# Attention with row maxima found ahead: another order of pieces, scores and sums in the unit loop, and one wait for each ACT and DVE instruction

## The chip, the cores and the metric

The kernel runs on one core of a Trainium2 chip. The metric is the time of one execution in device microseconds (us). The engines are named as in the profile: PE is TensorE's matmuls, PEld its weight loads, DVE is VectorE, ACT is ScalarE, POOL is GpSimd, SP is the engine that issues most DMAs. Each engine runs its own instructions in order, and they wait for each other by semaphores.

## What is computed

One block of a transformer with a layer norm in front of two branches: attention with 16 heads of 16 dimensions over 4096 positions in 2 batch rows, and a feed-forward branch with butterfly transforms. Cut to what matters:

```python
# x: (2, 4096, 256), W_qkv: (256, 768)
xn = layernorm(x)
qkv = (xn @ W_qkv + b_qkv).reshape(B, D, 3, 16, 16).transpose(2, 0, 3, 1, 4)
q, k, v = qkv
scores = softmax(einsum("bhip,bhjp->bhij", q, k), axis=-1)     # 32 x 4096 x 4096
attn = einsum("bhij,bhjp->bhip", scores, v).reshape(B, D, 256)
h = butterfly(xn @ W_exp + b_exp, up_weights)                  # 1024 wide, 10 stages
h = gelu(h + up_bias)
y = butterfly(h, down_weights) @ W_con + b_con + down_bias
return x + attn + y
```

The softmax subtracts the true maximum of each row, so the kernel needs each row's maximum before it can take the exponentials.

## The kernel before

**Stages.** First come the layer norm, q, k and v (to about 270 us), then the attention, which holds over 85% of the time, then the feed-forward branch from about 5294 us. The change touches the attention alone.

**Tiles and units.** The queries of a head are taken 2048 at a time (`QB`); there are 64 such rounds (`SUPER`). A round is worked on twice. As 16 *tiles* of 128 queries it goes through the search for maxima: q times all 4096 keys in 8 *pieces* of 512 keys (`PIECES`), each a matmul into one bank of PSUM. As 16 *units* it goes through the softmax proper: each unit multiplies two blocks of 128 keys (half 0 and half 1) with the 2048 queries in 8 *scores* of 512 columns (`score`, L843), ACT takes their exponentials (`exp`, L646), and PE multiplies these with v (`sums`, L857, four matmuls for each half, each run as two instructions). The maxima are ahead of the units by 21 tiles (`AHEAD`), so the loop over 1024 units does in step u the pieces of tile n = u + 21, the scores of unit u + 1 and the sums of unit u. The first 18 tiles (`PAIRED`) are done in another way ahead of the loop; the last 21 units have no pieces.

**Pieces.** DVE reduces a piece to its maximum over 512 keys (`reduce_piece`, L708). To save DVE one piece in eight, one bank holds a *difference*: q times (last keys of one half less those of another), matmul with `k_diff`. ACT takes its relu into `spill` (`rectify`, L670), and DVE adds that to the *merged* piece while it reduces it (L704): a + relu(b - a) is the larger of both. `DIFFERENCE` and `MERGED` say at which places of `PIECE` these stand (3 and 6 before; the difference at place 3 is that of the next tile, n + 1). A piece has 48 rows and a score 50, so each lies in the upper or the lower half of the PE array (`lower`), and two matmuls of different halves run side by side. The sums use all 128 rows.

**Banks.** Four banks hold scores in turn (a score waits for the exponential four before it), three banks hold pieces in turn (`use`, `bank_of`, `free_region`): each piece waits until the use three before it has been read. One bank holds the sums.

**Order in a step of PE before** (lines 885 to 905): piece 0, score 0, piece 1, scores 1 and 2, piece 2, score 3, sums of half 0; then the difference of the next tile, piece 4, scores 4 and 5, piece 5, scores 6 and 7, the merged piece 6, piece 7, sums of half 1. ACT's order is four exponentials, a relu, four exponentials. `SCORE` gives each score its half and its 512 queries. The engines' orders are written out by hand; no planner is at work.

**Once in 16 steps.** When a round's maxima are complete, DVE negates them and splits them into two bf16 parts (`negate`, `high_part`, `low_part`, L723, L728, L732) in the tile with n % 16 = 1, PE transposes them at n % 16 = 2 (`neg_to_rows`, L830; it takes a turn of the three banks), DVE copies them (`copy_rows`, L741) and SP places them under q. When a round's sums are complete, DVE transposes them behind the tile with n % 16 = 4 (`turn`, L747), and takes a reciprocal in the next (`invert`, L751); POOL scales and adds.

**Waits.** An instruction of ACT or DVE that waits for two semaphores is preceded by an instruction that waits for the first alone. Before, that is so for the exponentials of the first 512 queries of each half (sums of two units ago, then the score), for the relu (the merged piece of two tiles ago, then the difference) and for the merged reduction (the relu, then the piece).

Of the kernel before, what the change touches and what calls it, by code (L numbers as in the profile page):

```python
# [44 lines left out]
def attention_and_butterfly_ffn(nc, x, w_qkv, b_qk_columns, b_v, w_exp, b_exp, up_planes, up_bias_columns, down_planes,  # L45
# [13 lines left out]
    QG = QB // BANK  # L59
# [8 lines left out]
    UNITS = KT // 2  # L68
# [21 lines left out]
    with ExitStack() as ctx:  # L90
# [350 lines left out]

        PIECE = [(1, 0), (1, 1), (0, 0), (1, 2), (0, 1), (0, 2), (1, 3), (0, 3)]
        DIFFERENCE, MERGED = 3, 6


        SCORE = [(r // 2 % 2, 2 * (r // 4) + r % 2) for r in range(2 * QG)]
        LAST_OF_HALF = [max(r for r in range(2 * QG) if SCORE[r][0] == h) for h in range(2)]

# [13 lines left out]
        for n in range(PAIRED):  # L462
            for i in range(0, PAIRS_OF_TILE, 2):
                for what in ("apart", "second"):
                    for pair in (i, i + 1):
                        use((n, what, pair), what == "second")
        use((PAIRED, DIFFERENCE), False)
        for n in range(PAIRED, TILES_ALL + TURN_TILE + 1):
            if n % QT == TURN_TILE:
                use(("neg", n // QT - 1), True)  # L470
            for j in range(PIECES if n < TILES_ALL else 0):
                if j != DIFFERENCE:
                    use((n, j), True)
                elif n + 1 < TILES_ALL:
                    use((n + 1, j), False)
        vector_uses, scalar_uses = list(accumulate(by_vector)), list(accumulate(by_scalar))
# [40 lines left out]
        with nc.Block() as block:  # L517
# [122 lines left out]
            def _(act):  # L640
                def exp(u, r):
                    half, g = SCORE[r]
                    if g == 0 and u >= 2:
                        act.wait_ge(s_pv, 2 * (u - 2) + half + 1)
                    act.wait_ge(s_score, 2 * QG * u + r + 1)
                    nc.scalar.activation(probs[:, 2 * (u % 2) + half, BANK * g:BANK * g + BANK],  # L646
                                         ps_s[:, r % 4, :], ACT.Exp).then_inc(s_exp, 1)
# [18 lines left out]
                def rectify(n):  # L666
                    act.wait_ge(s_diff_ps, spilled(n))
                    if n >= PAIRED + 2:
                        act.wait_ge(s_region_free, vector_uses[use_of[n - 2, MERGED]])
                    nc.scalar.activation(spill[:, n % 2, :], region(use_of[n, DIFFERENCE]), ACT.Relu).then_inc(s_spilled, 1)  # L670
# [7 lines left out]
                act.wait_ge(s_ones_in, 16 * 4)  # L678
                for r in range(QG):
                    exp(0, r)  # L680
                rectify(AHEAD)
                for r in range(QG, 2 * QG):
                    exp(0, r)
                for u in range(UNITS_ALL):
                    if u + 1 < UNITS_ALL:
                        for r in range(QG):
                            exp(u + 1, r)
                    if u + AHEAD + 1 < TILES_ALL:
                        rectify(u + AHEAD + 1)
                    if u + 1 < UNITS_ALL:  # L690
                        for r in range(QG, 2 * QG):
                            exp(u + 1, r)

            @block.vector
            def _(dve):
                def reduce_piece(n, j):
# [4 lines left out]
                    if j == MERGED:  # L701
                        dve.wait_ge(s_spilled, spilled(n))
                        dve.wait_ge(s_region, vector_uses[use])
# [75 lines left out]
            def _(pe):  # L779
# [27 lines left out]
                def piece(n, j):  # L807

                    if j == DIFFERENCE:
                        n += 1  # L810
                    if n >= TILES_ALL:
# [35 lines left out]
                def sums(u, half):  # L847

                    s, at = divmod(u, UNITS)
                    head = s // 2  # L850
                    if at == 0 and half == 0:
                        if s > 0:
                            pe.wait_ge(s_o_free, s)
                        pe.wait_ge(s_vc[head % 2], 16 * (head // 2 + 1))
                    pe.wait_ge(s_exp, 2 * QG * u + LAST_OF_HALF[half] + 1)
                    for g in range(QG):
                        last = nc.tensor.matmul(ps_o[VW * g:VW * g + VW, :], v_cols[:, KT * (head % 2) + UNITS * half + at, :],  # L857
                                                probs[:, 2 * (u % 2) + half, BANK * g:BANK * g + BANK],
                                                start=(at == 0 and half == 0), stop=(at == UNITS - 1 and half == 1))
                    last.then_inc(s_pv, 1)  # L860
# [3 lines left out]
                for n in range(PAIRED):  # L864
                    for i in range(0, PAIRS_OF_TILE, 2):
                        pairs(n, i)
                piece(PAIRED - 1, DIFFERENCE)
                for n in range(PAIRED, AHEAD):
# [15 lines left out]
                for u in range(UNITS_ALL):  # L884
                    n = u + AHEAD
                    if n % QT == TURN_TILE and n // QT <= SUPER:
                        neg_to_rows(n // QT - 1)
                    piece(n, 0)
                    score(u + 1, 0)
                    piece(n, 1)  # L890
                    score(u + 1, 1)
                    score(u + 1, 2)
                    piece(n, 2)
                    score(u + 1, 3)
                    sums(u, 0)
                    piece(n, 3)
                    piece(n, 4)
                    score(u + 1, 4)
                    score(u + 1, 5)
                    piece(n, 5)  # L900
                    score(u + 1, 6)
                    score(u + 1, 7)
                    piece(n, 6)
                    piece(n, 7)
                    sums(u, 1)

# [235 lines left out]
```

## Time and profile before

| | |
|---|---|
| runs | 5672.61 us median of 3 (5670.88 to 5674.43) |
| profiled execution | 5674.86 us, of which the span of instructions is 5673.1 us |
| PE, DVE, ACT busy | 5605.1 (99%), 4884.6 (86%), 4977.2 (88%) us |
| POOL busy | 524.8 us (9%) |
| exponentials (L646) | 8192 x 608 ns, 4222.6 us busy |
| reductions (L708) | 6036 x 686 ns, 3966.7 us busy |
| merged reductions (L704) | 1006, 684.8 us busy |
| relus (L670) | 1006 x 597 ns, 601.0 us busy |
| granted TensorE clock | mean 0.992 of full |

A group's busy time is less than its count times its mean, since an engine begins an instruction before the last has quite ended: exponentials in a row start some 0.48 us apart though each takes 0.61. A busy PE is a PE that has some matmul under way, which says little of how full it is. By slices of the span, all three engines are at 90% or more from the third or fourth fortieth to the thirty-seventh: the attention looks the same from end to end.

### The profile page before, as it was taken

What the parts mean: (1) busy time and instruction counts of PE and PEld (TensorE: products, weight loads), DVE (VectorE), ACT (ScalarE), POOL (GpSimd) and SP (SyncE); (2) the same over time, 40 slices, a digit from 0 to 9 for tenths busy, and PEclk for the clock granted to TensorE, in tenths of its full rate; (3) what the DMA queues carried; (4) which work ended last, traced back from release to release, by engine and by line L of the source; (5) the groups of instructions that cost most, each with busy time, mean ns of one, the idle gap of its engine ahead of it and who ended that gap; (6) DMA issues with size and microseconds to landing.
All of it is one profiled execution on the core that took longest, in us unless ns stands there. A gap on an engine that the chain in (4) does not pass through costs nothing. (4 is left out here: it accounts for less than half of the span.)

```text
span 5673.1 us, 97332 instructions
## 1 busy us (share of the span) xinstructions
PE 5605.1 (99%) x35880; PEld 2613.5 (46%) x35880; DVE 4884.6 (86%) x9104; ACT 4977.2 (88%) x9651; POOL 524.8 (9%) x482
## 2 busy tenths in 40 slices
PE   8799999999999999999999999999999999999999
PEld 5444444444444444444444444444444444444698
DVE  6689999999999999999999999999999999996233
ACT  3489999999999999999999999999999999999544
POOL 2245564000000000000000000000000000000000
PEclk9889999999999999999999999999999999999999
DMA  8611111000000000000000000000000000000111
GB/s 288 200 43 43 50 54 42 21 21 19 14 16 21 21 21 21 15 21 21 21 18 14 16 21 21 21 20 16 21 21 21 17 12 20 21 21 2 34 44 41
DMA packets 232761, 197.02 MB, mean 35 GB/s; under 512 B 171752, under 2 KB 192616, under 8 KB 220520
## 3 DMA queue, kind: packets, MB, share of 16 engines
q1 hardware_dynamic: 228848, 168.00, 10.4%
q0 software_dynamic: 3456, 23.07, 1.4%
q8 instruction: 268, 4.39, 0.3%
q14 instruction: 189, 1.55, 0.1%
HBM read 128.07 MB, written 60.82 MB: 33 GB/s over the span
## 5 line engine op out<-in xcount | busy, mean ns | idle before, releaser
L646 ACT ACTIVATE probs<-psum 128x512 f32<-128x512 f32 x8192 | 4222.6, 608 | 294.8 <-PE psum L843 292.8
L708 DVE TENSOR_REDUCE maxima<-psum 128x1 f32<-128x512 f32 x6036 | 3966.7, 686 | 364.7 <-PE psum L821 255.6
L821 PE MATMUL psum<-k_rows,q_rows 48*128 48x512 f32 x7042 | 2494.3, 455 | 0.6 <-ACT spill L670 0.6
L857 PE MATMUL psum<-probs,v_cols 128*32 128x512 f32 x16384 | 2184.7, 605 | 0.5
L843 PE MATMUL psum<-q_rows,k_rows 50*128 50x512 f32 x8192 | 2061.2, 424 | 0.0
L821 PEld LDWEIGHTS psum<-k_rows,q_rows 48*128 48x128 f32 x7042 | 1176.6, 184 | 1248.8 <-DVE maxima L704 809.6
L843 PEld LDWEIGHTS psum<-q_rows,k_rows 50*128 50x128 f32 x8192 | 1266.5, 186 | 135.0 <-ACT probs L646 44.5
L704 DVE CUSTOM_DVE_ANT_0 merged<-psum,spill 128x512 bf16<-128x512 f32 x1006 | 684.8, 681 | 2.7 <-issue 1.9
L670 ACT ACTIVATE spill<-psum 128x512 f32<-128x512 f32 x1006 | 601.0, 597 | 23.9 <-PE psum L821 23.6
L857 PEld LDWEIGHTS psum<-probs,v_cols 128*32 128x32 f32 x16384 | 323.3, 108 | 622.0 <-issue 325.8
L821 PEld LDWEIGHTS psum<-k_diff,q_rows 48*128 48x128 f32 x1006 | 184.6, 183 | 843.0 <-DVE maxima L708 787.7
L821 PE MATMUL psum<-k_diff,q_rows 48*128 48x512 f32 x1006 | 498.5, 496 | 0.2 <-DVE maxima L708 0.2
L583 POOL TENSOR_TENSOR o_t<-o_t,recip 128x256 f32<-128x256 f32 x64 | 39.6, 618 | 4527.8 <-DVE recip L751 4527.8
L1049 ACT ACTIVATE gelus<-psum,bias_up 128x512 f32<-128x512 f32 x128 | 88.3, 690 | 189.4 <-PE psum L1013 187.6
L296 ACT ACTIVATE parts<-psum,bqk 128x512 fp32r<-128x512 f32 x64 | 59.0, 922 | 133.8 <-PE psum L406 102.6
L1091 DVE TENSOR_TENSOR hidden_low<-gelus,hidden_high 128x512 fp32r<-128x512 f32 x128 | 88.6, 692 | 100.9 <-ACT hidden_high L1052 100.9
L406 PE MATMUL psum<-xnt,wqkv 128*128 128x512 f32 x256 | 121.3, 619 | 29.7 <-DVE parts L345 28.5
L1025 PE MATMUL psum<-w_down_high,hidden_low 128*128 128x256 f32 x512 | 145.0, 283 | 0.0
L1025 PE MATMUL psum<-w_down_low,hidden_high 128*128 128x256 f32 x512 | 145.0, 283 | 0.0
L1025 PE MATMUL psum<-w_down_high,hidden_high 128*128 128x256 f32 x512 | 144.9, 283 | 0.0
L1097 DVE TENSOR_TENSOR y<-psum,y 128x1024 f32 (+1 forms) x16 | 19.6, 1225 | 125.0 <-PE psum L1025 125.0
L747 DVE STREAM_TRANSPOSE o_t<-psum 128x512 f32<-128x512 f32 x64 | 45.2, 706 | 74.8 <-PE psum L857 74.8
(94 smaller groups left out, 2067.0 us busy)
## 6 DMA issues: line engine op xcount, KB each, us to landing
q_rows<-q_parts SPq DMA_DIRECT2D x128, 256.0 KB
q_parts<-parts SPq DMA_DIRECT2D x32, 512.0 KB, 6.0
k_parts<-parts SPq DMA_DIRECT2D x32, 512.0 KB, 3.7
k_rows<-k_parts SPq DMA_DIRECT2D x64, 256.0 KB
q_rows<-q_parts SPq DMA_DIRECT2D x128, 128.0 KB
planes<-in_up_planes POOLq DMA_DIRECT2D x10, 1024.0 KB, 11.3
planes<-in_down_planes POOLq DMA_DIRECT2D x10, 1024.0 KB, 5.4
y<-in_x SPq DMA_DIRECT2D x16, 512.0 KB, 6.0
```

The source lines that it names most:

```text
L296: nc.scalar.activation(in_chunk_order(m, parts[:, PARTS * m, :]), from_chunk(m), ACT.Identity, bias=bqk[:, m:m + 1]).then_inc(s_high, 1)
L406: last = nc.tensor.matmul(ps_qk[:, m, :], wqkv[:, k, P * m:P * m + P], xnt[:, KD * p + k, :], start=(k == 0), stop=(k == KD - 1))
L646: nc.scalar.activation(probs[:, 2 * (u % 2) + half, BANK * g:BANK * g + BANK], ps_s[:, r % 4, :], ACT.Exp).then_inc(s_exp, 1)
L670: nc.scalar.activation(spill[:, n % 2, :], region(use_of[n, DIFFERENCE]), ACT.Relu).then_inc(s_spilled, 1)
L704: nc.vector.tensor_tensor_reduce(merged[:, :], region(use), spill[:, n % 2, :], 1.0, LOWEST, ALU.add, ALU.max, accum_out=largest).then_inc ...
L708: nc.vector.tensor_reduce(largest, region(use), axis=AX_X, op=ALU.max).then_inc(s_region_free, 1)
L821: nc.tensor.matmul(region(use_of[n, j]), q_rows[m % 4][lower:lower + ROWS, P * t:P * t + P], keys[lower:lower + ROWS, :], start=True, stop ...
L843: nc.tensor.matmul(ps_s[:, r % 4, :], k_rows[s // 2 % 2][lower:lower + ROWS + MAX_PARTS, key:key + P], q_rows[s % 4][lower:lower + ROWS + ...
L857: last = nc.tensor.matmul(ps_o[VW * g:VW * g + VW, :], v_cols[:, KT * (head % 2) + UNITS * half + at, :], probs[:, 2 * (u % 2) + half, BAN ...
L1025: last = nc.tensor.matmul(ps_d[:, t, 0:D], h[:, m, P * t:P * t + P], w[:, m, :], start=(m == 0 and n == 0), stop=(m == HT - 1 and n == 2))
L1049: nc.scalar.activation(gelus[:, m % 2, :], ps_h[:, m % 4, :], ACT.Gelu, bias=bias_up[:, 1, m:m + 1]).then_inc(s_h, 1)
L1091: nc.vector.tensor_tensor(hidden_low[:, m, :], gelus[:, m % 2, :], hidden_high[:, m, :].bitcast(F32), ALU.subtract).then_inc(s_h_low, 1)
```

## The change

Three things are altered, all in the attention.

The order within a step of the unit loop: the difference stands first and belongs to the same tile (`DIFFERENCE` is 0), so a step is difference, pieces 1 and 2, scores 0 to 3, pieces 3 and 4, sums of half 1; then piece 5, scores 4 and 5, the merged piece 6, piece 7, scores 6 and 7, sums of half 0. `SCORE` now takes the halves in turn, half 1 first, and `PIECE` is permuted to match. ACT's order is the relu and then eight exponentials.

The waits: the exponential no longer waits for the sums of two units ago, the relu no longer for the merged reduction of two tiles ago, the merged reduction no longer for the relu. In the new order PE issues the score behind those sums, the difference behind a piece that waited for that merged reduction, and the merged piece behind a piece that waited for the relu.

The sums of unit u start their accumulation with half 1 and end it with half 0.

```diff
--- before.py
+++ after.py
@@ -439,11 +439,11 @@
         ps_o = psum[:, 7, :]
 
 
-        PIECE = [(1, 0), (1, 1), (0, 0), (1, 2), (0, 1), (0, 2), (1, 3), (0, 3)]
-        DIFFERENCE, MERGED = 3, 6
-
-
-        SCORE = [(r // 2 % 2, 2 * (r // 4) + r % 2) for r in range(2 * QG)]
+        PIECE = [(1, 2), (0, 0), (1, 0), (1, 1), (0, 1), (0, 2), (1, 3), (0, 3)]
+        DIFFERENCE, MERGED = 0, 6
+
+
+        SCORE = [(1 - r % 2, r // 2) for r in range(2 * QG)]
         LAST_OF_HALF = [max(r for r in range(2 * QG) if SCORE[r][0] == h) for h in range(2)]
 
 
@@ -464,15 +464,11 @@
                 for what in ("apart", "second"):
                     for pair in (i, i + 1):
                         use((n, what, pair), what == "second")
-        use((PAIRED, DIFFERENCE), False)
         for n in range(PAIRED, TILES_ALL + TURN_TILE + 1):
             if n % QT == TURN_TILE:
                 use(("neg", n // QT - 1), True)
             for j in range(PIECES if n < TILES_ALL else 0):
-                if j != DIFFERENCE:
-                    use((n, j), True)
-                elif n + 1 < TILES_ALL:
-                    use((n + 1, j), False)
+                use((n, j), j != DIFFERENCE)
         vector_uses, scalar_uses = list(accumulate(by_vector)), list(accumulate(by_scalar))
 
         def region(n):
@@ -640,8 +636,6 @@
             def _(act):
                 def exp(u, r):
                     half, g = SCORE[r]
-                    if g == 0 and u >= 2:
-                        act.wait_ge(s_pv, 2 * (u - 2) + half + 1)
                     act.wait_ge(s_score, 2 * QG * u + r + 1)
                     nc.scalar.activation(probs[:, 2 * (u % 2) + half, BANK * g:BANK * g + BANK],
                                          ps_s[:, r % 4, :], ACT.Exp).then_inc(s_exp, 1)
@@ -665,8 +659,6 @@
 
                 def rectify(n):
                     act.wait_ge(s_diff_ps, spilled(n))
-                    if n >= PAIRED + 2:
-                        act.wait_ge(s_region_free, vector_uses[use_of[n - 2, MERGED]])
                     nc.scalar.activation(spill[:, n % 2, :], region(use_of[n, DIFFERENCE]), ACT.Relu).then_inc(s_spilled, 1)
 
                 minus_k()
@@ -676,19 +668,13 @@
                 for n in range(PAIRED, AHEAD):
                     rectify(n)
                 act.wait_ge(s_ones_in, 16 * 4)
-                for r in range(QG):
-                    exp(0, r)
-                rectify(AHEAD)
-                for r in range(QG, 2 * QG):
+                for r in range(2 * QG):
                     exp(0, r)
                 for u in range(UNITS_ALL):
+                    if u + AHEAD < TILES_ALL:
+                        rectify(u + AHEAD)
                     if u + 1 < UNITS_ALL:
-                        for r in range(QG):
-                            exp(u + 1, r)
-                    if u + AHEAD + 1 < TILES_ALL:
-                        rectify(u + AHEAD + 1)
-                    if u + 1 < UNITS_ALL:
-                        for r in range(QG, 2 * QG):
+                        for r in range(2 * QG):
                             exp(u + 1, r)
 
             @block.vector
@@ -699,7 +685,6 @@
                     column = COLUMNS * (n % QT) + j - (j > DIFFERENCE)
                     largest = maxima[:, n // QT % 2, column:column + 1]
                     if j == MERGED:
-                        dve.wait_ge(s_spilled, spilled(n))
                         dve.wait_ge(s_region, vector_uses[use])
                         nc.vector.tensor_tensor_reduce(merged[:, :], region(use), spill[:, n % 2, :], 1.0, LOWEST,
                                                        ALU.add, ALU.max, accum_out=largest).then_inc(s_region_free, 1)
@@ -806,8 +791,6 @@
 
                 def piece(n, j):
 
-                    if j == DIFFERENCE:
-                        n += 1
                     if n >= TILES_ALL:
                         return
                     m, t = divmod(n, QT)
@@ -848,7 +831,7 @@
 
                     s, at = divmod(u, UNITS)
                     head = s // 2
-                    if at == 0 and half == 0:
+                    if at == 0 and half == 1:
                         if s > 0:
                             pe.wait_ge(s_o_free, s)
                         pe.wait_ge(s_vc[head % 2], 16 * (head // 2 + 1))
@@ -856,7 +839,7 @@
                     for g in range(QG):
                         last = nc.tensor.matmul(ps_o[VW * g:VW * g + VW, :], v_cols[:, KT * (head % 2) + UNITS * half + at, :],
                                                 probs[:, 2 * (u % 2) + half, BANK * g:BANK * g + BANK],
-                                                start=(at == 0 and half == 0), stop=(at == UNITS - 1 and half == 1))
+                                                start=(at == 0 and half == 1), stop=(at == UNITS - 1 and half == 0))
                     last.then_inc(s_pv, 1)
 
                 pe.wait_ge(s_k[0], 16 * K_LOADS)
@@ -864,7 +847,6 @@
                 for n in range(PAIRED):
                     for i in range(0, PAIRS_OF_TILE, 2):
                         pairs(n, i)
-                piece(PAIRED - 1, DIFFERENCE)
                 for n in range(PAIRED, AHEAD):
                     if n == QT + TURN_TILE:
                         neg_to_rows(0)
@@ -885,24 +867,21 @@
                     n = u + AHEAD
                     if n % QT == TURN_TILE and n // QT <= SUPER:
                         neg_to_rows(n // QT - 1)
-                    piece(n, 0)
-                    score(u + 1, 0)
-                    piece(n, 1)
-                    score(u + 1, 1)
-                    score(u + 1, 2)
-                    piece(n, 2)
-                    score(u + 1, 3)
-                    sums(u, 0)
+                    for j in range(3):
+                        piece(n, j)
+                    for r in range(QG):
+                        score(u + 1, r)
                     piece(n, 3)
                     piece(n, 4)
+                    sums(u, 1)
+                    piece(n, 5)
                     score(u + 1, 4)
                     score(u + 1, 5)
-                    piece(n, 5)
+                    piece(n, 6)
+                    piece(n, 7)
                     score(u + 1, 6)
                     score(u + 1, 7)
-                    piece(n, 6)
-                    piece(n, 7)
-                    sums(u, 1)
+                    sums(u, 0)
```

## Rows read from the trace of the kernel before

**Rows 1.** Waits of the whole span: engine, line, releaser: us in total, times, longest.
```profile
PEld psum L821 <- DVE maxima L708: 830.2, 1097, 1.7
...
PEld psum L821 <- ACT spill L670: 354.7, 939, 1.1
...
ACT probs L646 <- PE psum L843: 292.8, 1005, 1.8
```

**Rows 2.** Busy time in four stretches of a unit (length, then each engine).
```profile
3004.15:3005.90 1.75, 1.75 (x14) 1.02 (x10) 1.47 (x3) 1.75 (x5) 0.00 (x0) 1.00 0.00 0
3005.90:3006.90 1.00, 1.00 (x11) 0.16 (x10) 1.00 (x4) 1.00 (x3) 0.00 (x0) 1.00 0.00 0
3006.90:3008.03 1.13, 1.13 (x12) 0.72 (x8) 1.01 (x2) 0.85 (x3) 0.00 (x0) 1.00 0.00 0
3008.03:3009.02 0.99, 0.99 (x9) 0.15 (x8) 0.99 (x3) 0.99 (x4) 0.00 (x0) 1.00 0.00 0
```

**Rows 3.** Timeline, first stretch: start, us, engine, line, operation [idle before].
```profile
3004.16 0.50 PE L821 MATMUL psum<-k_diff,q_rows 48*128 48x512 f32 x1
...
3004.69 0.60 ACT L670 ACTIVATE spill<-psum 128x512 f32<-128x512 f32 x1
3004.73 0.69 DVE L708 TENSOR_REDUCE maxima<-psum 128x1 f32<-128x512 f32 x1 [0.28 <-PE psum L821]
...
3005.34 0.31 PEld L821 LDWEIGHTS psum<-k_rows,q_rows 48*128 48x128 f32 x2 [0.39 <-ACT spill L670]
...
3005.47 0.50 PE L821 MATMUL psum<-k_rows,q_rows 48*128 48x512 f32 x1
```

**Rows 4.** Timeline of the rest of that unit.
```profile
3006.01 0.68 DVE L704 CUSTOM_DVE_ANT_0 merged<-psum,spill 128x512 bf16<-128x512 f32 x1
...
3006.62 2.69 DVE L708 TENSOR_REDUCE maxima<-psum 128x1 f32<-128x512 f32 x4
...
3006.90 0.50 PE L843 MATMUL psum<-q_rows,k_rows 50*128 50x512 f32 x1
...
3007.52 0.60 ACT L646 ACTIVATE probs<-psum 128x512 f32<-128x512 f32 x1 [0.28 <-PE psum L843]
3007.70 0.39 PE L843 MATMUL psum<-q_rows,k_rows 50*128 50x512 f32 x1
```

**Rows 5.** Timeline where maxima are negated and turned, DVE and PE.
```profile
1929.00 0.26 DVE L723 TENSOR_REDUCE neg_max<-maxima 128x16 f32<-128x112 f32 x1
...
1929.77 0.16 DVE L728 CAST neg_parts<-neg_max 128x16 bf16<-128x16 f32 x1
1929.94 0.69 DVE L708 TENSOR_REDUCE maxima<-psum 128x1 f32<-128x512 f32 x1
...
1932.00 0.22 PE L830 MATMUL psum<-ident_bf,neg_parts 128*32 128x128 bf16 x1
1932.15 0.49 PE L821 MATMUL psum<-k_rows,q_rows 48*128 48x512 f32 x1
...
1932.58 0.50 PE L821 MATMUL psum<-k_rows,q_rows 48*128 48x512 f32 x1
```

**Rows 6.** Timeline where a round's sums are transposed, DVE and PE.
```profile
2025.36 0.71 DVE L747 STREAM_TRANSPOSE o_t<-psum 128x512 f32<-128x512 f32 x1
2025.99 1.25 DVE L708 TENSOR_REDUCE maxima<-psum 128x1 f32<-128x512 f32 x2
2027.16 0.23 DVE L751 RECIPROCAL recip<-o_t 128x16 f32<-128x16 f32 x1
...
2027.15 0.49 PE L821 MATMUL psum<-k_diff,q_rows 48*128 48x512 f32 x1
2027.29 0.49 PE L821 MATMUL psum<-k_rows,q_rows 48*128 48x512 f32 x1
```

**Rows 7.** Line 830: count, duration ns min/median/max, first and last start.
```profile
L830 PE MATMUL psum<-ident_bf,neg_parts x64: 218/219/286, 284.7 to 5213.2; 128*32 128x128 bf16 x64
```

**Rows 8.** Timeline at the start of the loop, PE.
```profile
298.46 0.80 PE L821 MATMUL psum<-k_rows,q_rows 48*128 48x512 f32 x2 [0.56 <-ACT spill L670]
```

## The prediction

> **What bounds the kernel now.** I began with the page. PE shows 99%, but its matmuls overlap, so that share says little. ACT (88%) and DVE (86%) come near their limit without reaching it: neither is full. So I went to the table of waits [rows 1]. PE's weight loads wait for DVE's reductions and for ACT's relu; ACT and DVE in turn wait for PE. That is a ring, not one full engine, and one must see which link closes it. Most of the span is 1024 units of 4.87 us, nearly all alike, and a table of busy time over one of them, cut where PE changes its work, shows the ring [rows 2]: 1.75 us for the stretch that begins with the difference piece, 1.00 for a block of sums, 1.13 for the other stretch of pieces and scores, 0.99 for the other sums. Reader: the two sums blocks and the 1.13 us stretch are PE's own time; only the 1.75 us stretch holds a wait.
>
> Inside that stretch [rows 3]: the difference and piece 4 start at 3004.16, DVE starts on piece 4 at 3004.73 (0.57 later), takes 0.69, and 0.05 after its end, at 3005.47, PE starts the last piece, which needed that bank. The sums follow 0.43 later. 0.57 + 0.69 + 0.05 + 0.43 = 1.74. The relu makes a shorter ring beside it: start 3004.69, end 3005.29, piece 6 at 3005.34. The other stretch has four matmuls deep in each half of the array and no live wait; its last matmul, at 3007.70, is followed by the sums 0.32 later [rows 2, 4]. PE's cycle thus has one round trip to DVE in it, and DVE and ACT have two idle spells each.
>
> **The change, part by part. The order in a steady unit.** Call the start of the difference 0. The new stretch A is difference, piece 1, piece 2, four scores, pieces 3 and 4, sums(u, 1); stretch B is piece 5, four scores, pieces 6 and 7 among them, sums(u, 0). There are three banks for eight pieces, so each piece still waits for the one three before it: piece 3 for the relu, piece 4 for the reduction of piece 1. With the durations of rows 3: relu from 0.53 to 1.13, piece 3 at 1.19; reduction of piece 1 from 0.57 to 1.26, piece 4 at 1.31, sums at 1.74. These are the same numbers as now, since the same pair starts the stretch and the same round trip closes it. The sums take 1.00: B starts at 2.74. In B the longer half of the array holds pieces 5 and 7 and two scores, four deep as now: 1.13, sums at 3.87, next unit at 4.86. **Steady gain: nothing**, as long as the waits in B stay covered. DVE's starts are 0.60 to 0.61 apart when it doesn't wait [rows 4] (2.69 less 0.69, less a wait of some 0.2, over three; and 3006.01 to 3006.62), so it takes pieces 1 to 4 at 0.57, 1.17, 1.78 and 2.38, and the last is free at 3.12. Piece 7 wants its bank at about 3.21 if it isn't to come late (its turn in B gives an end at 3.71, and a matmul that waited needs 0.50 [rows 3]). The cover is 0.09 to 0.10 us. Now the same bank has far more: that is the new weak point. The other waits: DVE reaches piece 7 at 4.48 and frees its bank at 5.17, which is 0.31 into the next unit, so piece 2 and the scores behind it start some 0.1 late; the first exponential then starts at 1.10 and the fourth ends near 3.16, 0.2 ahead of the last score of B, which needs it. Nothing of that reaches the sums. A wait missed by d here costs 1003 times d.
>
> **The waits left out.** ACT loses the wait on the sums ahead of the first column block of each half and the wait on a merged piece ahead of the relu, DVE loses the wait on the relu ahead of the merged reduction. Where the instruction isn't starved, the trace gives them no time: DVE's merged reduction follows 0.60 after the reduction ahead of it [rows 3, 4]. Where ACT is starved they show: the first exponential starts 0.12 after its score ends (3006.90 + 0.50 against 3007.52), the relu, whose extra wait was over long before, 0.03 to 0.04 after its matmul [rows 3, 4]. The difference, some 0.06 to 0.09, lies in ACT's idle time (0.28 there [rows 4]), which PE doesn't wait for. So I put it at 0 in the 1003 units with pieces. In the last 21 units, which have no pieces, ACT and PE wait for each other in one ring and it counts once each: 21 x 0.06 = 1.2 us gained; between 0 and 1.9. The Trainium skill, "VectorE: DVE Perf Modes", in "The DRAIN you can't avoid", says that a semaphore with each operation costs nothing extra. By it the last units gain 0, not 1.2 us; for back-to-back work the trace agrees (0.60 with and without the extra wait), for an instruction that is starved it doesn't.
>
> **The stops, once in 16 units.** Here the order matters. (a) Negation of the maxima. Two of DVE's three small operations, the negation and the first split, fall between piece 0 and piece 4; the split's slot is 0.17 (1929.77 to 1929.94), and I take as much for the negation [rows 5]. DVE would idle 0.28 ahead of piece 4 anyway [rows 3], so they are nearly hidden. In the new order they fall between the reductions of pieces 1 and 4, with no idle spell between. Piece 4's bank comes free at 3.12 + 0.34 = 3.46, 0.25 past what piece 7 can bear: that unit is 0.25 longer. (b) The next unit. The transposes take PE 0.15 [rows 5] in either order. Now they cost 0.24 in all: the second piece is at 0.43 after the first (1932.15 to 1932.58) and not 0.34, as it waits for the reduction of the tile before. In the new order that reduction runs late after (a), to 0.18 into this unit, so piece 1 can be loaded at 0.24 and everything that hangs on its round trip is 0.23 late. DVE's copy of the turned rows fits ahead of piece 1. Together 0.48 against 0.24: **0.24 lost**. (c) The transposition of the sums takes a DVE slot of 0.63 [rows 6] (2025.36 to 2025.99). It now falls in DVE's two idle spells: what is left is the 0.14 by which the piece beside the difference is late (2027.15, 2027.29 [rows 6]), some 0.12 in the unit. In the new order it comes between piece 7 and piece 1 of the next tile: slot from 5.09 (0.23 of the next unit) to 0.86, where piece 1 would have been taken at 0.57. A piece that has waited reads a little faster there (two reductions in 1.25 [rows 6]), so piece 4 is 0.24 to 0.29 late; the reciprocal's 0.16 behind piece 1 takes the rest of the cover, 0 to 0.1 more. Taken 0.25, against 0.12: **0.13 lost**. The unit that holds each of these has pieces in 62 of the 64 rounds [rows 7]. 62 x (0.24 + 0.13) = 23 us. Bounds: 62 x 0.1 = 6 us if most is caught up by DVE's idle spells, 62 x 0.55 = 34 us if the backlog costs two units each time.
>
> **The start.** Now one relu of a coming tile is queued behind four exponentials, and PE idles 0.56 us for it [rows 8]. With the difference at the head of its own tile that stall goes, and the relu then queues behind eight exponentials at the first unit, where PE is late at a low clock anyway. Between 3 gained and 1 lost; I take 1 gained. SP's queue isn't moved: its loads wait on counts of exponentials and sums that come in the same units as now.
>
> **The sum**, against the profiled execution: span 5673.1 + 23 - 1.2 - 1 = 5693.9; around the span lie 1.8 us (5674.86), so 5695.7. This execution is 2.3 us over the median of the runs shown (5672.61), which gives a median of **5694 us**, +0.4%.
>
> **The rivals.** (1) No change to measure: the stops are mostly absorbed, since DVE idles 0.6 us in a steady unit in either order, and the start and the tail give 2 back. 5673 + 6 - 2 = 5677. For it: DVE catches up within one unit. Against: the wait for piece 7 comes before DVE's second idle spell. (2) Faster: the extra waits matter in every unit. Mechanism: the last score of stretch A now starts 0.1 late because it waits for the fourth exponential, and the exponentials start late by the extra wait. If it is this link, and not DVE's, that sets the last piece, 0.06 comes back in each of 1003 units: 5673 - 60 + 23 = 5636; with half of it, 5666. It decides if piece 7 now starts by that score and not 0.05 after DVE's reduction; rows 3 speak against it, as the 0.05 is exact. (3) Much slower: the cover of 0.1 for piece 7 isn't there in the steady unit. The price is 1003 us for each us missed: 0.05 gives 5694 + 50 = 5744. It decides if the first four reductions of a unit are ever more than 0.64 apart or the first starts later than 0.67. For it: the cover is small and my starts are good to 0.02 or 0.03 each. (4) The change doesn't take the order it says: excluded, the diff writes each engine's order out.
>
> **How the numbers follow.** Chances: forecast 0.56 (own range 5685 to 5707), rival 1 0.19, rival 2 0.15, rival 3 0.10. 0.2% of 5673 is 11 us, about what a measurement of this kernel can tell from no change: the line is at 5661 and 5684. Rival 1 is within, a third of rival 2 too, with a few hundredths of the forecast's low end: same 0.25. Slower 0.63, faster 0.12. The range: 5660 takes in rival 1 and the weak end of rival 2, 5728 the upper bound of the stops and the weak end of rival 3; about 0.19 is left out, most of it below.
>
> **What would show it.** In the changed trace a steady unit should last 4.86 us, with sums 1.74 and 3.87 after the difference. DVE should idle about 0.3 ahead of piece 1 and 0.3 ahead of piece 5. PE's idle time for the reductions should gather at the last piece of A. The relu should no longer have scores or exponentials between its matmul and it. ACT should start 0.04 after a score that it waited for, not 0.12. The rounds of 16 units should be 78.5 us apart instead of 78.1. If a steady unit differs from 4.86 by more than 0.02, the main step is wrong: longer by a wait of piece 7 means rival 3, shorter means that PE's ring isn't what I took it for. If the unit holds and the rounds stay at 78.1, rival 1 is right.

## The result, and the profile after

The changed kernel takes 5689.64 us (median of 9 runs, 5686.55 to 5691.74) against 5672.61 (median of 9, 5668.83 to 5674.91): 17 us more, ratio 1.0030, 95% interval 1.0021 to 1.0039. The prediction was 5694.

| us | before | after |
|---|---|---|
| span of the profiled execution | 5673.1 | 5687.8 |
| start of the last matmuls of the sums | 5288.9 | 5303.1 |
| mean unit, 1500 to 4500 us | 4.884 | 4.902 |
| PE, DVE, ACT busy | 99%, 86%, 88% | 99%, 85%, 90% |

What comes behind these takes 384 to 385 us in both. So 14 of the 14.7 us between the two spans lie ahead of that point, and the change touches only the attention.

The waits of the whole span (engine, line, releaser: us in total, times, longest), against [rows 1]:

```profile
PEld psum L804 <- DVE maxima L693: 1054.7, 2141, 1.7
...
PEld psum L804 <- ACT spill L662: 277.4, 942, 0.6
...
ACT probs L640 <- PE psum L826: 36.1, 128, 1.5
```

PE waits more for DVE, and ACT hardly idles for scores any more: 36 us instead of 293. The kernel got slower all the same, so that idle time had cost nothing.

A steady unit of the changed kernel, cut in the same four stretches as [rows 2]:

```profile
3230.07:3231.81 1.74, 1.74 (x14) 1.03 (x10) 1.48 (x3) 1.71 (x5) 0.00 (x0) 1.00 0.00 0
3231.81:3232.80 0.99, 0.99 (x9) 0.15 (x8) 0.99 (x3) 0.99 (x3) 0.00 (x0) 1.00 0.00 0
3232.80:3233.93 1.13, 1.13 (x11) 0.67 (x7) 0.92 (x2) 1.03 (x3) 0.00 (x0) 1.00 0.00 0
3233.93:3234.93 1.00, 1.00 (x10) 0.16 (x9) 1.00 (x4) 1.00 (x4) 0.00 (x0) 1.00 0.00 0
```

1.74, 0.99, 1.13, 1.00: the four lengths of before. Its timeline (start, us, engine, line, operation), against [rows 3] and [rows 4]:

```profile
3230.07 0.50 PE L804 MATMUL psum<-k_diff,q_rows 48*128 48x512 f32 x1
...
3230.61 0.60 ACT L662 ACTIVATE spill<-psum 128x512 f32<-128x512 f32 x1
3230.64 2.48 DVE L693 TENSOR_REDUCE maxima<-psum 128x1 f32<-128x512 f32 x4 [0.26 <-PE psum L804]
3231.20 3.25 ACT L640 ACTIVATE probs<-psum 128x512 f32<-128x512 f32 x6
...
3231.81 1.07 PE L840 MATMUL psum<-probs,v_cols 128*32 128x512 f32 x8
...
3233.34 0.69 DVE L693 TENSOR_REDUCE maxima<-psum 128x1 f32<-128x512 f32 x1 [0.21 <-PE psum L804]
...
3233.93 0.64 PE L840 MATMUL psum<-probs,v_cols 128*32 128x512 f32 x4
```

The relu starts 0.54 after the difference, the first reduction 0.57. DVE does four reductions in one go (2.48, so 0.60 apart) and is done with piece 4 at 3233.12, 3.05 into the unit; it then idles until piece 5 is there.

Most of the loss must then be in the stops, as the prediction calls what happens once in 16 units. The interval from each difference matmul to the next, averaged over rounds 10 to 62, by the place in its round of the tile to which the first of the two belongs (computed from all the starts):

| interval that begins at n % 16 = | 1 | 2 | 4 | 5 | 6 | each other, about | a round |
|---|---|---|---|---|---|---|---|
| before | 4.867 | 5.096 | 4.863 | 4.880 | 4.980 | 4.861 | 78.152 |
| after | 5.056 | 5.027 | 4.865 | 5.110 | 4.860 | 4.865 | 78.430 |

### The profile page after: what moved, and what is told of

The parts are those of the page before. It is cut to its first block and busy times, and to the rows that moved or that the text cites. A ratio compares the mean times of both kernels' runs of the same rounds, so it can differ in the third digit from the quotient of the medians.

```text
span 5687.8 us, 93278 instructions
## 1 busy us (share of the span) xinstructions
PE 5621.0 (99%) x35880; PEld 2550.0 (45%) x35880; DVE 4812.8 (85%) x9104; ACT 5119.0 (90%) x9651; POOL 525.3 (9%) x482
## 5 line engine op out<-in xcount | busy, mean ns | idle before, releaser
L693 DVE TENSOR_REDUCE maxima<-psum 128x1 f32<-128x512 f32 x6036 | 3892.5, 684 | 452.9 <-PE psum L804 445.6
L826 PE MATMUL psum<-q_rows,k_rows 50*128 50x512 f32 x8192 | 2220.5, 422 | 0.0
L826 PEld LDWEIGHTS psum<-q_rows,k_rows 50*128 50x128 f32 x8192 | 1195.1, 185 | 68.3 <-ACT probs L640 44.4
```

Source lines behind the costliest of these rows:

```text
L693: nc.vector.tensor_reduce(largest, region(use), axis=AX_X, op=ALU.max).then_inc(s_region_free, 1)
L826: nc.tensor.matmul(ps_s[:, r % 4, :], k_rows[s // 2 % 2][lower:lower + ROWS + MAX_PARTS, key:key + P], q_rows[s % 4][lower:lower + ROWS + ...
```

## The experiments

Each is timed beside the kernel before on the same chip; the interval of a ratio is 95%.

**The waits alone, and the order alone.**

```diff
 # old order, waits out
-                    if g == 0 and u >= 2:
-                        act.wait_ge(s_pv, 2 * (u - 2) + half + 1)
...
-                    if n >= PAIRED + 2:
-                        act.wait_ge(s_region_free, vector_uses[use_of[n - 2, MERGED]])
...
-                        dve.wait_ge(s_spilled, spilled(n))
```

> The old order with the three waits left out (sums ahead of the exponentials, merged piece ahead of the relu, relu ahead of the merged reduction). My theory: in the 1003 units with pieces an extra wait lies in ACT's idle time and is worth nothing; in the last 21 units it counts once each, 0.06 us, so 5672.6 - 1.2 = 5671. Rival: the waits count in every unit, 5672.6 - 60 = 5613. A first exponential that waits for its score should start 0.04 us after the score's end and not 0.12.

5669.05 us, ratio 0.9994 (0.9985 to 1.0003): no change that can be told, and not the 60 us of the rival. The first exponential of the second stretch now starts 0.07 us after its score's end, where it was 0.13 (medians over all such exponentials; 0.04 was expected). ACT idles 231 us for scores instead of 293, and PE doesn't wait for what was gained.

```diff
 # new order, waits back
+                    if g == 0 and u >= 2:
+                        act.wait_ge(s_pv, 2 * (u - 2) + (1 - half) + 1)
...
+                    if n >= PAIRED + 2:
+                        act.wait_ge(s_region_free, vector_uses[use_of[n - 2, MERGED]])
...
+                        dve.wait_ge(s_spilled, spilled(n))
```

> The new order with the three waits put back, so the order alone. My theory: the tail gives 1 us back, 5689.6 + 1 = 5691, all the rest of the +17 us is the order's. Rival: the new order needs the lean waits, 5690 + 30 to 60 = 5720 to 5750.

5689.15 us, ratio 1.0031 (1.0019 to 1.0042), as the changed kernel itself. The loss belongs to the order. So does the fall of ACT's idle time, which is 36 us here too.

**Without the stops.** Both kernels leave out the negation, the split, the turning and the copy of the maxima in all rounds but the first, and the transposition of the sums, the reciprocal and what POOL does with them in all but the first and last; PE, DVE and SP wait on counts to match.

```diff
-            if n % QT == TURN_TILE:
+            if n == QT + TURN_TILE:
                 use(("neg", n // QT - 1), True)
...
-                        if 0 < m <= SUPER and t == 1:
+                        if m == 1 and t == 1:
...
-                    if n % QT == TURN_TILE and n // QT <= SUPER:
-                        neg_to_rows(n // QT - 1)
...
-                    if s >= 0 and u == QT - 1:
+                    if s in (0, SUPER - 1) and u == QT - 1:
                         turn(s)
```

> The old order without what happens once in 16 units: negation, split, turning and copying of the maxima are done in the first round alone, transposition and reciprocal of the sums in the first and last alone. My theory: the stops cost the old order 0.39 us a round by its trace (78.16 against 16 x 4.86), so 5672.6 - 62 x 0.39 = 5649. Rival (the stops are not where the kernels differ): the two kernels without stops differ by 17 us as the full ones do.

> The new order without the same work as in the run before it (maxima handled in the first round alone, sums transposed in the first and last alone). My theory: its stops cost 0.59 us a round (78.43 against 16 x 4.865), so 5689.6 - 62 x 0.59 = 5653, only 4 us over the old order without stops, from a steady unit that is 0.004 longer, less 2 at the start and the tail. Rival: 17 us over it, 5666.

5649.99 (0.9960, 0.9947 to 0.9974) and 5653.24 us (0.9966, 0.9954 to 0.9978). The 17 us have shrunk to 3, within the intervals of each other. The difference matmuls between 1500 and 4500 us, with their count and their first and last start, first in the old order without stops, then in the new one (one fence for each kernel):

```profile
L823 PE MATMUL psum<-k_diff,q_rows x617: 491/492/500, 1502.6 to 4499.5; 48*128 48x512 f32 x155
```

```profile
L806 PE MATMUL psum<-k_diff,q_rows x617: 491/498/502, 1500.7 to 4497.2; 48*128 48x512 f32 x155
```

2996.9 / 616 = 4.865 and 2996.5 / 616 = 4.864 us a unit: in these two executions the orders are equally fast. That most of the 17 us comes from the stops is thus shown. That all of it does is not: the profiled execution of the old order took 5653.21 us, 3 more than its median, and its median unit is 4.860 us against 4.866 in the new order, the same few ns as with the stops. Up to 6 us may belong to the order of the steady unit.

**The small operations moved behind piece 4.**

```diff
-                            if j == 1:
+                            if j == 4:
                                 negate(m - 1)
-                            if j == 2:
+                            if j == 5:
                                 high_part(m - 1)
-                            if j == 4:
+                            if j == 6:
                                 low_part(m - 1)
```

> The new order with negation, first and second split behind the reductions of pieces 4, the one behind it and the merged one, so that nothing small is ahead of piece 4. My theory: the unit with n % 16 = 1 loses its wait for piece 7 (5.055 to 4.90 us), but DVE comes 0.15 later to the end of that tile, and in the next unit piece 1, whose bank now waits for it, is later still (5.03 to 5.29): 0.11 more in a round, 5690 + 7 = 5697. Rival: the small operations vanish in the idle spell, 0.15 less in a round, 5680.

5699.47 us, ratio 1.0046 (1.0033 to 1.0060), so 10 us over the changed kernel. The interval at n % 16 = 1 fell from 5.056 to 4.945, that at 2 rose from 5.027 to 5.267. DVE's backlog doesn't vanish in the idle spell; it is handed to the next unit, whose piece 1 waits for this tile's last reduction.

**The cover of piece 7.** An added copy of 128x16 on DVE, in tiles of the unit loop.

```diff
                             reduce_piece(n, j)
+                            if j in (1, 2) and n >= AHEAD:      # or: j == 2; or: j in (3, 4)
+                                nc.vector.tensor_copy(extra_out[:, j % 2, :], extra_in[:, :])
```

> The new order, and in each tile of the unit loop DVE does two added copies of 128x16, behind the reductions of pieces 1 and 2, which is ahead of piece 4's. My theory: a small copy on a busy DVE takes a slot of 0.07 to 0.08 us (the first split takes 0.073 there), two take 0.15; piece 7's bank has a cover of 0.10, so each of 1003 units is 0.05 longer: 5690 + 50 = 5740 (0 at least, 75 at most). Rival: DVE idles 0.6 us in a unit, so nothing changes, 5690.

> As the run before it with one added copy, behind the reduction of piece 2. My theory: 0.075 fits into the cover of 0.10, so 5690 to 5695 (a stop gets a little longer each, some 62 x 0.07 = 4 us). If the cover were less than I think, 5700 or more; a slope without any cover would give 5690 + 75 = 5765.

> The new order with the same two added copies behind the reductions of pieces 3 and 4. The first lies ahead of piece 4's reduction, the second in the idle spell ahead of piece 5. My theory: 0.075 within the cover and 0.075 in the idle spell, nothing in a steady unit: 5690 to 5695. Rival (DVE's added busy time counts wherever it stands): as with both ahead, 5740.

> The old order with two added copies behind the reductions of pieces 1 and 2, ahead of DVE's idle spell of 0.28. My theory: both lie in the idle spell, 5673 to 5680. Rival: the old order has as little cover as the new one, 5673 + 50 = 5723.

The times missed all four expectations: 5866.69 (ratio 1.0343, 1.0326 to 1.0360), 5763.21 (1.0159, 1.0142 to 1.0176), 5827.15 (1.0266, 1.0249 to 1.0283) and 5808.66 us (1.0208, 1.0162 to 1.0255; three of its four runs took 5806 to 5811 us, one 5758). The units say where. By median over the whole loop they are 4.926, 4.872, 4.871 and 4.861 us, where 4.865 + 0.05, 4.865, 4.865 and 4.861 were expected: the steady unit does what the theory says. But in rounds 2 to 8 a round takes 94.3, 86.3, 94.4 and 94.7 us instead of 78.4 or 78.1, 55 to 116 us too much in seven rounds; afterwards 79.58, 78.73, 79.03 and 78.45. Those early rounds are the ones in which POOL folds the feed-forward weights (it is done near 1000 us). The added copies of the kernel with one copy, first up to 1000 us, then from 1100 to 5000 (count: ns min/median/max):

```profile
L755 DVE CAST extra_out<-extra_in x131: 165/331/4072, 300.0 to 996.5; 128x16 bf16<-128x16 f32 x131
...
L755 DVE CAST extra_out<-extra_in x793: 164/165/268, 1100.7 to 4997.5; 128x16 bf16<-128x16 f32 x199
```

A copy of 0.165 us takes up to 4 us while POOL works. Of the 131 early copies, 61 overlap no instruction of POOL, and the longest of these takes 0.167 us; the median of the other 70 is 0.54 (from all starts and ends). The four of 4 us begin while POOL issues a DMA and last through three of its 1.28 us operations. No run takes POOL's work away.

TensorE's granted clock fell in those rounds as well. Busy time in that stretch (length, then each engine, the granted clock, DMA), first in the kernel before, then in the old order with copies:

```profile
360.00:1020.00 660.00, 660.00 (x4336) 282.86 (x4332) 612.14 (x1135) 619.31 (x1216) 357.08 (x299) 1.00 0.17 46
```

```profile
360.00:1020.00 660.00, 625.72 (x3578) 259.42 (x3574) 594.45 (x1155) 513.25 (x1004) 337.44 (x283) 0.88 0.15 42
```

The granted clock is 1.00 in the kernels before and after, and 0.94, 0.98, 0.91 and 0.88 in the four with copies. In the kernel with one copy it falls to its lower level within 2 us of the end of each of the four longest copies, in which PE stands still for more than half the time (the first of these copies, then a stretch behind it):

```profile
407.45:411.50 4.05, 1.70 (x12) 0.42 (x11) 4.05 (x3) 2.40 (x5) 3.99 (x4) 1.00 0.71 259
413.00:419.00 6.00, 6.00 (x24) 2.20 (x28) 3.68 (x9) 3.25 (x7) 5.84 (x5) 0.50 0.02 4
```

The run of 5758 us had a mean clock of 0.988, the three near 5809 us 0.978 to 0.980. So held-up copies and a lower clock both stand in this loss; how much belongs to each was not separated.

From there on, in a unit with two copies ahead (DVE's rows of that kernel):

```profile
3379.20 0.69 DVE L695 TENSOR_REDUCE maxima<-psum 128x1 f32<-128x512 f32 x1 [0.31 <-PE psum L809]
3379.81 0.17 DVE L755 CAST extra_out<-extra_in 128x16 bf16<-128x16 f32 x1
3379.88 0.68 DVE L695 TENSOR_REDUCE maxima<-psum 128x1 f32<-128x512 f32 x1
3380.48 0.17 DVE L755 CAST extra_out<-extra_in 128x16 bf16<-128x16 f32 x1
3380.56 2.03 DVE L695 TENSOR_REDUCE maxima<-psum 128x1 f32<-128x512 f32 x3
```

Each copy takes a slot of 0.07 to 0.08. Two make 0.15 and the unit grows by 0.06; one makes 0.075 and the unit grows by 0.00 to 0.01: a cover of about 0.09, as worked out in the prediction. The old order takes both in its idle spell in the steady unit. At the stops neither order has cover left: a later round with one copy is 78.73 against 78.43, 0.3 longer, where I had allowed 0.07.

**The second matmul of a pair.**

```diff
 # new order
-        PIECE = [(1, 2), (0, 0), (1, 0), (1, 1), (0, 1), (0, 2), (1, 3), (0, 3)]
-        DIFFERENCE, MERGED = 0, 6
+        PIECE = [(0, 0), (1, 2), (1, 0), (1, 1), (0, 1), (0, 2), (1, 3), (0, 3)]
+        DIFFERENCE, MERGED = 1, 6
...
-                    if t == 0 and j == DIFFERENCE:
+                    if t == 0 and j == 0:
 # old order
-        PIECE = [(1, 0), (1, 1), (0, 0), (1, 2), (0, 1), (0, 2), (1, 3), (0, 3)]
-        DIFFERENCE, MERGED = 3, 6
+        PIECE = [(1, 0), (1, 1), (0, 0), (0, 1), (1, 2), (0, 2), (1, 3), (0, 3)]
+        DIFFERENCE, MERGED = 4, 6
```

> The new order with piece 0 ahead of the difference in the pair that starts a stretch. In the trace whatever waits for the second matmul of such a pair starts 0.03 us later than what waits for the first (0.568 against 0.534). The round trip to DVE closes the unit, so my theory gives 0.03 less in each of 1003 units: 5690 - 30 = 5660, less if the cover of piece 7 shrinks with it (5660 to 5670). Rival: the 0.03 are DVE's own delay against ACT's, or the sums are set by PE, no change: 5690.

> The old order with piece 4 ahead of the difference in the same way. My theory: 0.03 less in each of 1003 units, with cover to spare: 5673 - 30 = 5643. Rival: no change, 5673.

> As the run before it with the three extra waits left out. My theory: the waits are worth 1 us in the tail, 5642. Rival: with the round trip shorter, ACT's extra wait closes the unit and leaving it out is worth up to 0.06 a unit more.

New order: 5656.66 us, ratio 0.9973 (0.9963 to 0.9984), 33 us less than the changed kernel. Old order: 5654.5 us, 0.9969 (0.9957 to 0.9981), 17 us less than before where 30 were expected. Old order with the waits out as well: **5640.6 us, 0.9944 (0.9931 to 0.9958)**, the fastest of all, 31 us under the kernel before. The steady unit is 4.835, 4.828 and 4.827 us: 0.03 gained in each, so the round trip to DVE does close the unit. In the old order it comes through whole only without the waits: a late round is 77.86 with them and 77.65 without, 0.21 x 62 = 13 us, and nearly all of that stands in the intervals at n % 16 = 2 (5.175 against 5.089) and 5 (5.093 against 4.990). DVE's rows around a stop, first with the waits, then without:

```profile
3245.57 0.69 DVE L708 TENSOR_REDUCE maxima<-psum 128x1 f32<-128x512 f32 x1
3246.25 0.69 DVE L704 CUSTOM_DVE_ANT_0 merged<-psum,spill 128x512 bf16<-128x512 f32 x1
3246.87 0.08 DVE L704 DVE_READ_ACCUMULATOR2_ANT maxima<- 128x1 f32 x1
```

```profile
3242.23 0.69 DVE L703 TENSOR_REDUCE maxima<-psum 128x1 f32<-128x512 f32 x1
3242.84 0.68 DVE L699 CUSTOM_DVE_ANT_0 merged<-psum,spill 128x512 bf16<-128x512 f32 x1
```

With the relu's wait ahead of it the merged reduction starts 0.68 behind the reduction before it, without it 0.61; so it is by median over all units. In these two kernels piece 6 has to wait for DVE's reduction of the piece that was moved ahead and no longer for the relu, and starts 1.28 after its pair instead of 1.18. It is then ready only just when DVE is, so the extra wait is live in every unit. (The run took out all three waits together; that this one is what counts is read from these rows.) A steady unit hides the 0.07; at a stop, where DVE's end of the tile is what the next unit's second piece waits for, it counts.

## Why the prediction was right, step by step

**The steady unit unchanged: right.** 1.74 and 3.86 for the sums were forecast as 1.74 and 3.87, 4.86 for the unit; medians are 4.860 before and 4.867 after, means outside the stops 4.861 and 4.865. The two orders of the first two experiments show the same (means 4.859 without the waits and 4.864 with them). These 4 to 6 ns make 4 to 6 us over 1003 units, which the forecast had at nothing; the kernels without stops neither confirm nor exclude them. The cover of piece 7 was forecast at 0.09 to 0.10: in the trace the bank is free at 3.05, the weight load can follow 0.05 later, and by the forecast's estimate it may come near 3.20. The kernels with added copies confirm it.

**The waits left out at nothing in the units: right for this change,** shown by the first two experiments. In the tail the forecast was 1.2 us; a unit there fell from 4.13 to 4.08 us, and with the waits alone taken out the stretch from unit 1003 to the last sums fell from 83.2 to 82.0. ACT's starved exponential won 0.06 as forecast, though it starts 0.07 behind its score and not 0.04. It wasn't right as a general statement: it held because the old order has slack around the merged reduction. With the round trip 0.03 shorter the same waits cost 13 us. The Trainium skill, "VectorE: DVE Perf Modes", "The DRAIN you can't avoid", has a semaphore with each operation cost nothing extra. The 0.68 against 0.61 above is a case where a second wait does cost, on an instruction whose input is ready no sooner than its engine.

**The stops: right in kind, too high in size, two terms of the sum wrong.** Forecast 23 us; a round grew by 78.430 - 78.152 = 0.28, 62 x 0.28 = 17 us, and 0.22 of it, 14 us, stands in the intervals with stops. The changed kernel's rows around the negation, PE and DVE, against [rows 5]:

```profile
3264.68 0.69 DVE L693 TENSOR_REDUCE maxima<-psum 128x1 f32<-128x512 f32 x1 [0.27 <-PE psum L804]
3265.29 0.26 DVE L708 TENSOR_REDUCE neg_max<-maxima 128x16 f32<-128x112 f32 x1
3265.47 0.68 DVE L693 TENSOR_REDUCE maxima<-psum 128x1 f32<-128x512 f32 x1
3266.07 0.17 DVE L713 CAST neg_parts<-neg_max 128x16 bf16<-128x16 f32 x1
3266.14 1.28 DVE L693 TENSOR_REDUCE maxima<-psum 128x1 f32<-128x512 f32 x2
```

```profile
3268.13 1.06 PE L840 MATMUL psum<-probs,v_cols 128*32 128x512 f32 x8
3269.01 0.22 PE L813 MATMUL psum<-ident_bf,neg_parts 128*32 128x128 bf16 x1
3269.16 0.49 PE L804 MATMUL psum<-k_diff,q_rows 48*128 48x512 f32 x1
3269.37 0.83 PE L804 MATMUL psum<-k_rows,q_rows 48*128 48x512 f32 x2
...
3271.08 1.06 PE L840 MATMUL psum<-probs,v_cols 128*32 128x512 f32 x8
```

(a) The two slots ahead of piece 4 were put at 0.17 each, 0.34 in all. The first split takes 0.07 (3266.07 to 3266.14), because DVE was busy: the 0.17 of [rows 5] held a wait for piece 4. So 0.25 less the cover gives 0.15, not 0.25. This was the mis-sized term. (b) The transposes cost PE not 0.15 but 0.03: they start 0.88 after the sums (3268.13 to 3269.01), so sums to next piece is 1.03 where it is 1.00 without. What costs is the turn of the banks they take: piece 1 now waits for the last reduction of the tile before and starts 0.21 after the difference (3269.16 to 3269.37) instead of beside it, and the sums follow at 1.92 instead of 1.74. In the old order the same turn cost 0.20 (0.43 between the pieces instead of 0.34, and a weight load no longer hidden). The two intervals: forecast 0.48, found 0.19 + 0.16 = 0.35. The old order's, forecast 0.24, measures 0.24. Loss 0.11 instead of 0.24. (c) The transposition of the sums: forecast 0.25 against 0.12, found 0.25 against 0.14, as in these rows, against [rows 6]:

```profile
3284.16 0.71 DVE L732 STREAM_TRANSPOSE o_t<-psum 128x512 f32<-128x512 f32 x1
3284.79 0.65 DVE L693 TENSOR_REDUCE maxima<-psum 128x1 f32<-128x512 f32 x1
3285.36 0.23 DVE L736 RECIPROCAL recip<-o_t 128x16 f32<-128x16 f32 x1
```

The reduction starts 0.85 after the unit's first matmul (3283.94) instead of 0.57. That is 0.28; it reads 0.04 faster, and 0.25 arrives at the unit. The rest of the 0.28 by which a round grew, 0.06, is the steady unit's 0.004, sixteen times.

**The start and the tail: sign and size right.** At unit 20 the changed kernel is 1.8 us ahead (second sums at 405.6 against 407.5), forecast 1. From there to unit 1003 it loses 16.8. From unit 1003 on it gains 0.9, forecast 1.2.

So 16.8 - 1.8 - 0.9 = 14.1 us by the end of the attention in the two traces. The medians are 17 us apart; the profiled execution of the kernel before was 2.3 us over its median, that of the changed one at it.

**Luck.** The forecast of 5694 against 5689.64 looks better than its terms. The stops came out 9 us below their 23, and 4 us that the forecast hadn't in it, from the steady unit, filled part of the gap.

**The rivals.** That the stops are absorbed fell: the three intervals that hold them in the new order are 0.16 to 0.25 longer than the rest, and without stops the 17 us shrink to 3. That the extra wait closes the unit fell for this change, and its mechanism turned up in another kernel. That piece 7 has no cover fell, with 0.09 measured. What stays open is whether the few ns by which a steady unit is longer are the order's own, and where in it they arise.

## What to carry to other kernels

In a ring of engines that is closed by one round trip, idle time on the others is cover: count it ahead of the point where it is needed, not over the unit, for a rare operation placed before that point costs its slot less the cover, and one placed after it hands its backlog to the next unit. Before reordering a loop, compare the chain that closes it, link by link; if it is the same, look for the difference in the rare steps. And look at which of two matmuls issued side by side the closing chain waits for: putting it first was worth twice what the change lost.

## What the runs showed of the hardware

Of two matmuls that start together in different halves of the array, the one issued second releases its reader 0.03 us later. In the kernel before the relu starts 0.53 behind its matmul, issued first, and the reduction 0.56 behind its own; with the two exchanged in the new order the relu starts at 0.57 and the reduction at 0.53 (medians). So it is the place in the pair and not the engine, and the exchange moved 0.03 us a unit. The Trainium skill, "TensorE: Matmul & The Clock Gate", in "The cost: per-tile semaphore tail", says that increments of side-by-side matmuls are served one after the other, some 26 ns each; the trace, with some 30 to 35 ns, agrees roughly.

A small copy on DVE with input and output in SBUF, fp32 to bf16, takes 0.165 us alone and up to 4.07 us while POOL works, with a median of 0.33 from 300 to 1000 us. One to two such copies a unit cost 55 to 116 us in seven rounds, the lower clock of these rounds included. The Trainium skill, "SBUF — State Buffer", in "SBUF: two separate sides", describes a port pair that GpSimd and some instructions of DVE hold in turn for a whole instruction, the other being blocked. That a copy is held agrees; that the longest outlasted three POOL operations in a row is more than one instruction's time. Whether this copy is of the kind that takes the pair, no run here shows by itself. The kernel's reductions read PSUM and write a column of SBUF; they take at most 0.694 us in those rounds as in the later ones.
